# A transformer block on one core: the columns of x are loaded ready laid out and normalised by GpSimd, and no longer transposed by TensorE

## What is computed

```python
x = x + tanh(g_xattn) * attention(layernorm(x), ctx, ctx)
x = x + tanh(g_ffn) * ffn(layernorm(x))

def layernorm(x):
    m = mean(x, axis=-1); v = var(x, axis=-1)
    return (x - m) / sqrt(v + 1e-5)

# attention: 16 heads x 4 channels x 16 features, q from layernorm(x), k and v from ctx
q = mix(layernorm(x) @ Wq.T + bq)
k = mix(ctx @ Wk.T + bk)
v = mix(ctx @ Wv.T + bv)
```

## Time and profile before

| | us |
|---|---|
| median of 3 runs | 1339.45 |
| lowest and highest | 1339.38, 1345.51 |
| the profiled execution, its own time | 1340.49 |
| its span, first to last instruction | 1338.7 |
| PE busy | 1320.3 |
| POOL busy | 567.5 |
| DVE busy | 703.7 |
| ACT busy | 409.5 |

### The profile page before, as it was taken

One profiled execution on the slowest core, in us unless ns is written; L12 is line 12 of the kernel. 1 busy time (PEld: TensorE's weight loads), 2 busy tenths in 40 slices (PEclk: granted clock), 3 DMA queues, 4 the chain that ended last, 5 costly groups with the idle time before them and its releaser, 6 DMA issues.

```text
span 1338.7 us, 22258 instructions
## 1 busy us (share of the span) xinstructions
PE 1320.3 (99%) x8352; PEld 1110.9 (83%) x8352; DVE 703.7 (53%) x1371; ACT 409.5 (31%) x743; POOL 567.5 (42%) x777
## 2 busy tenths in 40 slices
PE   8999999999999999999999999999999999999999
PEld 8888888888888888777888888888788888888887
DVE  6423433445855545576777777777875243253110
ACT  3312221111112222355565555555551120111100
POOL 1899999999800000446566665655500000000000
PEclk9999999999999999999999999999999999999999
DMA  7898736434447676999888887777442202211011
GB/s 250 252 313 220 195 80 205 157 142 166 148 149 182 166 184 157 284 277 258 229 237 232 231 231 224 223 220 218 179 174 111 79 23 88 79 63 63 32 42 53
DMA packets 188939, 228.17 MB, mean 170 GB/s; under 512 B 26528, under 2 KB 124960, under 8 KB 188832
## 3 DMA queue, kind: packets, MB, share of 16 engines
q1 hardware_dynamic: 162096, 188.07, 47.3%
q10 hardware_dynamic: 26736, 38.68, 9.8%
HBM read 141.74 MB, written 83.89 MB: 169 GB/s over the span
## 4 chain that ended last, share of the span: by engine, by line
PE 81%; POOL 12%; DMA 2%; SPq 1%; DVE 1%; issue 1%; ACT 0%; ACTq 0%; POOLq 0%; DVEq 0%
PE bank L160 17%; PE bank L161 17%; PE bank L162 17%; PE bank L1464 5%; POOL mixed_part L786 5%; PE bank L1484 4%; PE bank L1445 4%; PE bank L1446 4%; PE bank L1499 4%; PE bank L1447 4%; POOL mixed_sum L793 3%; PE bank L350 2%; POOL mixed_sum L786 2%; POOL value_in L793 2%; PE bank L1471 1%
## 5 line engine op out<-in xcount | busy, mean ns | idle before, releaser
L1650 DVE TRANSPOSE_TENSOR_REDUCE part<-bank 128x16 f32<-128x512 f32 x256 | 174.1, 692 | 2.9 <-PE bank L1464 0.5
L1596 ACT ACTIVATE probT<-bank 128x512 f32<-128x512 f32 x256 | 138.9, 595 | 88.4 <-PE bank L1484 84.9
L1266 DVE SCALAR_TENSOR_TENSOR raw_d<-bank,gates,raw_d 128x512 f32<-128x512 f32 x32 | 24.0, 750 | 162.8 <-PE bank L162 162.8
L1445 PE MATMUL bank<-w_hi,oT_hi 128*128 128x512 f32 x256 | 108.3, 423 | 1.2 <-POOL oT_lo L1763 1.2
L576 DVE SCALAR_TENSOR_TENSOR stage_lo<-bank,bias_mixed,stage_hi 128x512 fp32r<-128x512 f32 x46 | 34.4, 750 | 129.2 <-ACT stage_hi L578 129.2
L160 PE MATMUL bank<-place_a,w_hi 128*128 128x512 f32 x256 | 100.4, 392 | 1.0 <-DVE place_a L153 1.0
L160 PE MATMUL bank<-place_b,place_a 128*128 128x512 f32 x256 | 100.0, 391 | 0.9 <-DVE place_c L153 0.9
L160 PE MATMUL bank<-w_hi,yT_hi 128*128 128x512 f32 x256 | 100.9, 394 | 0.0
L1446 PE MATMUL bank<-w_lo,oT_hi 128*128 128x512 f32 x256 | 100.8, 394 | 0.0
L1447 PE MATMUL bank<-w_hi,oT_lo 128*128 128x512 f32 x256 | 100.5, 393 | 0.0
L161 PE MATMUL bank<-w_lo,yT_hi 128*128 128x512 f32 x256 | 99.7, 389 | 0.0
(11 more groups left out here) (241 smaller groups left out, 3075.8 us busy)
## 6 DMA issues: line engine op xcount, KB each, us to landing
k_rows<-stage_hi SPq DMA_DIRECT2D x128, 128.0 KB, 2.7
v_pad<-v_out SPq DMA_DIRECT2D x32, 512.0 KB, 2.6
v_place<-v_pad ACTq DMA_DIRECT2D x64, 256.0 KB, 4.2
tin<-in_ctx_cols SPq DMA_DIRECT2D x26, 512.0 KB, 4.4
k_in<-k_rows SPq DMA_DIRECT2D x64, 192.0 KB, 3.1
q_in<-q_rows SPq DMA_DIRECT2D x128, 96.0 KB, 3.3
q_rows<-wq_own SPq DMA_DIRECT2D x81, 128.0 KB, 2.5
raw_d<-x_mid SPq DMA_DIRECT2D x17, 512.0 KB, 3.4
```

Source lines behind the costliest of these rows:

```text
L1445: pe.matmul(o_bank[out][:], hi[:, c, :], wo_hi[:, k, cols], start=(k == 0), stop=False)
L1596: act.activation(probT[o % NPT][:, i].rearrange("k a p q -> k (a p q)"), two_bank[i][:], ACT.Exp).then_inc(s_exp, 1)
L1650: dve.tensor_reduce(part[o % NS][:, :, 2 * i:2 * i + 2, :].rearrange("k a p b -> k a (p b)"), one_bank[i][:].rearrange("k (a b t) -> k a b ...
```

## The change

x arrives a second time, as `x_cols`: for every batch its 1024 features as columns, 128 partitions by 8 chunks of 128 tokens, laid out before the launch as `ctx_cols` is. `x_jobs` has no PE part any more; it splits a tile of these columns. Tokens now run along the free dimension, so mean and inverse deviation of a token are no per-partition scalars. They are measured as before from the token-major tile (`x_measure`), written to DRAM (`put`: 128 partitions x 8 bytes), and read back onto all partitions (`get`: one row of 1 KB, 128 times). `normalise_x` then takes two tensor operations of 128x1024 with two inputs each: on DVE for batches 0 to 3, on POOL, behind the mixing of the weights, for batches 4 to 15. The tiles of columns lie in buffers that other data leave: for batches 0 to 3 those of mixed Wq chunks 1 to 4, for the others in that of the raw Wv (which is also `place_c`, read by the last value job). Measurements and splits are placed elsewhere in the order of jobs, and the splits of batch 3 stand ahead of the last value job.

```diff
-                    plan.append((free - 0.5, load))
+                    plan.append((free - 0.5 if n - 2 < CTX else measured_at[n - 2 - CTX] - 0.35, load))
...
+            MOMENTS_AFTER, first_get = 5, []
+
+            def x_tile(b):
+
+                i = b if b < GB else GB + (b - GB) % KC
+                return x_tiles[i], s_xcols[b % GB], 16 * (b // GB + 1)
+
+            def load_x_cols(b, at, free):
+
+                tile, landed, _ = x_tile(b)
+
+                def load(sp):
+                    free(sp)
+                    sp.dma_start(tile, x_cols[b]).then_inc(landed, 16)
+                plan.append((at, load))
+
+            def x_measure(b, job):
+
+                tile, landed = load_input(CTX + b)
+                own = own_moments[b % 2]
+                measured_at[b] = len(line.jobs)
+
+                def on_vector(dve):
+                    landed(dve)
+                    dve.bn_stats(x_stats[:, 0, :], tile[:, 0:HALF])
+                    link(dve.bn_stats(x_stats[:, 1, :], tile[:, HALF:D]))
+                    if b >= 2:
+                        dve.wait_ge(s_xput[b % 2], 16 * (b // 2))
+                    link(dve.bn_aggr(own[:], x_stats[:]))
+                    dve.tensor_scalar(x_var[:], own[:, 1:2], EPS, None, ALU.add).then_inc(s_xstat, 1)
+                    dve.wait_ge(s_xroot, b + 1)
+                    link(dve.reciprocal(x_rstd[:], x_root[:]))
+                    link(dve.tensor_tensor(x_tmp[:], x_rstd[:], x_rstd[:], ALU.mult))
+                    link(dve.tensor_tensor(x_tmp[:], x_tmp[:], x_var[:], ALU.mult))
+                    link(dve.tensor_scalar(x_tmp[:], x_tmp[:], -0.5, 1.5, ALU.mult, ALU.add))
+                    dve.tensor_tensor(own[:, 1:2], x_rstd[:], x_tmp[:], ALU.mult).then_inc(s_xrstd, 1)
+
+                def on_scalar(act):
+                    act.wait_ge(s_xstat, b + 1)
+                    act.activation(x_root[:], x_var[:], ACT.Sqrt).then_inc(s_xroot, 1)
+
+                def put(sp):
+                    sp.wait_ge(s_xrstd, b + 1)
+                    sp.dma_start(moments[b], own[:]).then_inc(s_xput[b % 2], 16)
+
+                def get(sp):
+                    sp.wait_ge(s_xput[b % 2], 16 * (b // 2 + 1))
+                    if b >= MOMENTS:
+                        sp.wait_ge(s_xnorm_dve, min(b - MOMENTS + 1, GB))
+                    if b >= MOMENTS + GB:
+                        sp.wait_ge(s_xnorm_pool, b - MOMENTS - GB + 1)
+                    if b < MOMENTS:
+                        sp.wait_ge(line.emptied, wq_end[MOMENTS_AFTER])
+                    sp.dma_start(all_moments[b % MOMENTS].rearrange("p t a -> p (t a)"),
+                                 moments[b].rearrange("t a -> (t a)").partition_broadcast(P)).then_inc(s_xget[b % MOMENTS], 16)
+                job.dve_pre, job.act_pre = on_vector, on_scalar
+                plan.append((measured_at[b] - 0.3, put))
+                if b:
+                    plan.append((measured_at[b] - 0.25, get))
+                else:
+                    first_get.append(get)
+
+            def normalise_x(eng, b, finish, done):
+
+                tile, landed, count = x_tile(b)
+                cols = tile.rearrange("p (k t) -> p k t", t=P)
+                mean, rstd = (all_moments[b % MOMENTS][:, :, a].unsqueeze(1).to_broadcast([P, KC, P]) for a in range(2))
+                eng.wait_ge(landed, count)
+                eng.wait_ge(s_xget[b % MOMENTS], 16 * (b // MOMENTS + 1))
+                finish(eng.tensor_tensor(cols, cols, mean, ALU.subtract))
+                eng.tensor_tensor(cols, cols, rstd, ALU.mult).then_inc(done, 1)
+
+            def x_normalised(eng, b):
+
+                if b < GB:
+                    eng.wait_ge(s_xnorm_dve, b + 1)
+                else:
+                    eng.wait_ge(s_xnorm_pool, b - GB + 1)
 
             def x_jobs(b):
-                hi, lo = x_place(b // GB)
-                t_end[CTX + b] = transpose_jobs(line, tin[b % 2], norm.done(b), hi[:, b % GB, :, :], lo[:, b % GB, :, :])
+
+                tile, _, _ = x_tile(b)
+                g = b // GB
+                to_hi, to_lo = x_place(g)
+                for half in range(2):
+                    cols, part = slice(half * HALF, (half + 1) * HALF), slice(4 * half, 4 * half + 4)
+                    hi = to_hi[:, b % GB, part, :].rearrange("p a b -> p (a b)")
+                    lo = to_lo[:, b % GB, part, :].rearrange("p a b -> p (a b)")
...
-                if n in (3, 4, 5):
-                    ring.release((1, 2, 0)[n - 3], end)
+                if n == MOMENTS_AFTER:
+                    plan.append((end + 0.2, first_get[0]))
+                if 1 <= n <= GB:
+                    load_x_cols(n - 1, end + 0.5, lambda sp: sp.wait_ge(line.emptied, end))
...
+                for b in range(GB, NB):
+                    normalise_x(pool, b, then, s_xnorm_pool)
...
-                if j >= NB - GB:
-                    x_norm(j - NB + GB, line.jobs[-1])
+                if j == NB - 1:
+                    x_measure(GB, line.jobs[-1])
                 if j in QUERY_AT:
                     query_chunk(QUERY_AT.index(j))
+                if j == NB - 1:
+                    x_jobs(GB - 1)
+                    line.jobs[-2].dve_pre = lambda dve: normalise_x(dve, GB - 1, link, s_xnorm_dve)
                 v_job(b, 1)
+                if NB - GB <= j + 1 < NB:
+                    x_measure(j + 1 - NB + GB, line.jobs[-1])
+                if NB - GB <= j < NB - 1:
+
+                    def normalise_then_measure(dve, b=j - NB + GB, measure=line.jobs[-1].dve_pre):
+                        normalise_x(dve, b, link, s_xnorm_dve)
+                        measure(dve)
+                    line.jobs[-1].dve_pre = normalise_then_measure
                 if j < NB - GB:
                     ctx_jobs(NB + j)
-                else:
+                elif j < NB - 1:
                     x_jobs(j - NB + GB)
+            ring.release(1, t_end[CTX + 2])
+            ring.release(2, t_end[CTX + 3])
+            values_end = len(line.jobs)
+
+            def values_read(sp, b):
+
+                line.wait_filled(sp, v_end[VALUE_ORDER[-1]])
+                sp.wait_ge(s_xnorm_dve, b - GB + 1)
+            for b in range(GB, 2 * GB):
+                load_x_cols(b, values_end + 0.3, lambda sp, b=b: values_read(sp, b))
 
...
-                        if c in (0, 2, 4, 5):
-                            x_norm((g + 1) * GB + (0, 2, 4, 5).index(c), job)
-                        if c in (1, 3, 5, 6):
-                            x_jobs((g + 1) * GB + (1, 3, 5, 6).index(c))
+                        if c in (0, 1, 3):
+                            x_measure((g + 1) * GB + 1 + (0, 1, 3).index(c), job)
+                        if c == 6 and g + 2 < NG:
+                            x_measure((g + 2) * GB, job)
+                        if c in (2, 4, 5, 6):
+                            b = (g + 1) * GB + (2, 4, 5, 6).index(c)
+                            x_jobs(b)
+                            if b + GB < NB:
+                                load_x_cols(b + GB, len(line.jobs) + 0.5, lambda sp, b=b: sp.wait_ge(line.emptied, t_end[CTX + b]))
```

64 lines of the change are left out of this document (46 added, 18 removed).

## The result

The changed kernel takes **1376.99 us** (median of 4 runs, 1374.26 to 1380.32) where the kernel before takes 1339.41 (1339.35 to 1345.51): ratio 1.0268, 95% interval 1.0245 to 1.0292. It is 2.7% slower; the forecast was 1338.9, with a range from 1330 to 1350. The profiled execution took 1380.32 us, its span is 1378.3, against 1338.7 before: 39.6 us to be found.

The account below looks back on a forecast made before the run. PE, busy 99% of the span, was taken as the bound. The terms -14.2 - 1.0 (an old wait gone) + 10 + 3 + 1.6 summed to -0.6 us, giving 1338.9 us, range 1330 to 1350.

Parts of the forecast that it names:

- Transposes, -14.2: In the query jobs, removing PE's transposes of x saves 0.89 us for each of 16 batches, 14.2 us.
- The boundary, +10: Between values and queries, PE waits about 10 us for DVE's chain to the split of batch 3; bounds 4 to 15.
- one wait of 1.4 us for moments: In DVE's chain at the end of the values, only batch 1's moments were expected to be waited for, 1.4 us.
- The banks' margin of 2 us: At the last value jobs, eight banks let PE go on despite late emptying, with about 2 us to spare.
- The queries through SP, +3: In the query groups, SP falls behind and moments of batches 15 and 11 come late, costing PE 3 us.
- I take 2.3: In the query groups, the moments' write was taken to land 2.3 us after its issue.
- rival 2: In the query groups, SP becomes the bound if a write lands in about 2.7 us or more: 13 us, 1348.9; chance 0.25.
- My own rule of 3 us for each 0.3 us of landing: In the queries, each 0.3 us more of write landing adds some 3 us over the two groups.
- the upper end of the landing, 3.2 us: For the moments' write in the queries, the slowest landing the range covered was 3.2 us, which costs 13 us.
- The clock, +1.6: Behind PE's long wait at the boundary, a lowered clock slows the first work by 1.6 us; bounds 0 and twice that.
- Rival 3, GpSimd beside VectorE: In the queries, POOL's long instructions hold up DVE's measurements and splits: 8 us at the groups, 1343.9; chance 0.1.
- Costed at nothing: In the queries, POOL's 62 us, the column loads, measurement-only passes and staging pairs' new waits were taken to cost nothing.

Follow-up runs that it names:

- x10: x8 with the moments' read moved directly behind the next load, ahead of that job's stores: 1333.03 us, ratio 0.9944 to the kernel before.
- x11: x2 with each batch measured ahead of the normalising of the batch before it at the end of the values: 1337.39 us, ratio 0.9966.
- x9: Changed kernel with the 512 KB load of the next rows issued behind the 1 KB write of the moments: 1369.73 us, ratio 1.0213.
- x2: Changed kernel with the moments' write issued on ScalarE's queue and SP's read moved behind that job's stores: 1347.57 us, ratio 1.0052.
- x12: Kernel before with only a 1 KB write and read-back through DRAM added for batches 4 to 15, data unused: 1361.31 us, ratio 1.0159.
- x3: Changed kernel with the moments' read taken from other DRAM data, not waiting for the write, which is still issued: 1339.46 us, ratio 0.9993.
- x4: Changed kernel with extra, overwritten matmuls keeping PE busy in the waits ahead of the four query groups: 1380.87 us, ratio 1.0306.
- x7: x2 with 44 extra, overwritten matmuls in PE's wait ahead of the first query product: 1345.28 us, ratio 1.0032.
- x8: x2 with batches 0 to 3 normalised as rows and transposed on PE as in the kernel before: 1335.70 us, ratio 0.9953.

## Why the prediction was wrong

- **Transposes, -14.2: right.** With no stand of SP or PE a group takes 43.5 us for 47.1, 3.6 for four batches. 12 of the 16, in x10, give 7.8 us by the medians, where 10.7 less 2.5 of waits is 8.2.
- **The boundary, +10: right in place, too small by about 4.6 us** (PE waited 13.2 + 1.4 = 14.6; bounds 4 to 15). Batch 0's normalising began at 343.33, forecast 343.2, but the queries at 390.3, forecast 385.3. The chain was mis-told in one respect: I summed DVE's work and one wait of 1.4 us for moments. DVE waited 2.44 + 1.33 + 2.00 = 5.8 us for those of batches 1 to 3, which is 4.4 of the 5.0 us. x11 shows that the order of measuring and normalising, which puts every round trip in series, is worth 7.6 us of PE's wait. The banks' margin of 2 us failed too: 1.35 us of wait ahead of a value job.
- **The queries through SP, +3: this is the step that failed,** by the term "I take 2.3" for the landing of the write. The mechanism was the forecast's and rival 2's, with the condition as stated: it decides from about 2.7 us. The write takes 4.7 in the median, and SP stands 18.3 us in group 1 where I had 6.8; its issuing, 39.7 us, is close to my 8 x 4.0 + 4 x 0.61 + 7.3 = 41.7. My own rule of 3 us for each 0.3 us of landing gives 3 + (4.7 - 2.3) / 0.3 x 3 = 27 us; the waits ahead of the three groups are 28.7. That they agree is in part luck: the rule was for two groups, and batch 7, which I had in time, is late by 6.5 us. Rival 2, at 13 us, had less than half of it too. The bound that failed is the upper end of the landing, 3.2 us: I took the nearest rows as bounds, and none of them is a write of 8 bytes a partition behind six stores and a load. A smaller slip: without the loads of columns a group costs SP 48.5 - 2.4 = 46.1 us, still 2.6 over, so the lag grows in group 2 as well.
- **Why the write lands so late is open.** It isn't its place behind the load alone (4.2 us without, x9), nor SP's queue (6.1 on ACT's, x2). From 385 to 545 us it goes roughly with how busy the DMA engines are: 4.8 us at a share of 0.59 (x12), 5.0 at 0.68 (the changed kernel), 7.3 at 0.88 (x2), 6.2 at 0.89 (x3); x9, 4.5 at 0.74, doesn't fit. But the stores of 128 KB beside it land in 3.2 us, so the traffic alone doesn't explain it either. A write of the same 1 KB in fewer, longer pieces is the rival that was not tried.
- **What the rule of the Trainium skill would have done.** The fixed cost of about 2.0 us ("DMA: Bandwidth & Descriptors" of the Trainium skill, the section on the anatomy of one DMA, which gives it for DMAs that GpSimd issues; this write is SP's) would have moved the sum the wrong way. The least landing here, 2.6 us, is not far from it; the median is 4.7.
- **The clock, +1.6.** The half clock was real and larger, 11 us of PE's work. x4 shows for group 0, and its unchanged time suggests for the rest, that it lay ahead of waits that something else set. The term is shown to matter only where no such wait follows (x7 against x2, about 3 us in group 0).
- **Rival 3, GpSimd beside VectorE.** The stretching is there, 2.9 us for a half split of 0.68, and with it the port rule of "SBUF — State Buffer", section "SBUF: two separate sides", of the Trainium skill agrees. It costs nothing in x3, where the same instructions run at 1339.5 us. It isn't always free: in x8 a stretched pair of splits, 5.07 us for 1.29, stands in the chain ahead of PE's wait of 4.71 us.
- **Costed at nothing:** the traffic and GpSimd's time were rightly so (x3). The staging pairs were not: 22.1 us of ACT's waiting, though no run shows what that is worth by itself.
- **Sum.** Measured against the forecast's terms: -14.2 - 1.0 + 13.2 + 1.4 at the boundary + 28.7 in the queries + 11 of clock = +39, in place of -0.6.

## What to carry to other kernels

A wait for a DMA's landing on a queue that also issues other work takes its whole landing time out of that queue each round, and a transfer of 1 KB is no exception. It costs nothing as long as issuing and standing together fit into the stage (group 0 of x12), and all that is over once they don't; so sum the two against the stage's time. Price the landing by a write of the same shape in the same traffic, not by the nearest row. If the sum is near the stage's time, let another engine issue the write, or put work of the same queue between write and read: that did not shorten the flight here, and won 17 to 31 of 38 us. Where a chain alternates a short producer with a consumer that waits for a round trip, run the producer one step ahead.

## What the runs showed that was not expected

- 1 KB from 128 partitions to DRAM took 2.6 us at the least, 4.7 in the median and 10.2 at the most on SP's queue, and 6.1 in the median on ACT's: a queue of its own did not make it faster. In the queries, stores of 128 KB landed sooner (3.2 us) than this 1 KB (5.0).
- Taking the 512 KB load from in front of it brought the median to 4.2 only (x9).
- VectorE's split of 128x512 from two SBUF inputs went from 0.68 us in the median to 2.92 at the most, beside GpSimd's operations of 2.43 us.
- A clock at half for 4.4 us behind the first wait had no price as long as something else set the end of the group: with the full clock group 0 was no shorter (x4).
